# LSTM gate biases as ScalarE operands, one tanh per gate, gate products in two PSUM banks, on a recurrent Trainium2 kernel

## The reference, cut to what matters

```
def _lstm_cell(xt, h, c, wih, whh, b):
    g = xt @ wih + h @ whh + b
    i, f, gg, o = jnp.split(g, 4, axis=1)
    c = sigmoid(f) * c + sigmoid(i) * tanh(gg)
    h = sigmoid(o) * tanh(c)

encoded = tanh(xt @ We + st @ Ue + be)
new_state = tanh(xt @ Wx + st @ Ws + bk)           # eight candidates
mem = concat([encoded, err], mem[:-1])
a = relu(mem.flat @ enc_w1 + enc_b1); agent_in = relu(a @ enc_w2 + enc_b2)
h1, c1 = _lstm_cell(agent_in, h1, c1, ...)         # cell 0 of the kernel
h2, c2 = _lstm_cell(h1, h2, c2, ...)               # cell 1 of the kernel
gate = softmax(h2 @ gate_w + gate_b) * theta + gs * (1 - theta)
st = sum_c gate_c * new_state_c; pred = clamp01(st[-1]); err = pred - yt
```

## Time and profile before

| what | value |
|---|---|
| runs, median (lowest to highest) | 5569.39 us (5567.42 to 5569.56), 3 runs |
| the profiled execution, span of its instructions | 5567.1 us |
| what lies around that span, against the median of the runs | 2.3 us |
| mean granted TensorE clock | 0.998 of full |
| busy: PE, DVE, ACT, POOL | 98%, 84%, 68%, 40% |
| chain that ended last: DVE, PE, ACT, issue | 54%, 19%, 17%, 8% |

### The profile page before, as it was taken

How to read it: one execution, slowest core, us unless ns; L and a number is a source line. 1 busy time by engine, 2 the same in 40 slices (tenths; PEclk the granted TensorE clock), 3 DMA queues, 4 the chain that set the end, 5 groups by cost and what they waited for, 6 DMA issues and landing times.

```text
span 5567.1 us, 187596 instructions
## 1 busy us (share of the span) xinstructions
PE 5448.0 (98%) x67584; PEld 3452.2 (62%) x67584; DVE 4654.7 (84%) x12848; ACT 3792.9 (68%) x9729; POOL 2203.7 (40%) x4101
## 2 busy tenths in 40 slices
PE   8999999999999999999999999999999999999998
PEld 5666666666666666666666666666666666666665
DVE  7888888888888888888888888888888888888887
ACT  5666666666666666666666666666666666666665
POOL 3344444433333344444443333334444444333333
PEclk9999999999999999999999999999999999999999
DMA  2111111111111111111111111111111111111111
GB/s 67 29 31 29 29 31 29 31 28 31 28 31 29 31 29 31 29 29 31 29 31 28 31 28 31 29 31 29 31 29 29 31 28 31 28 31 28 31 29 39
DMA packets 299285, 172.38 MB, mean 31 GB/s; under 512 B 156734, under 2 KB 263882, under 8 KB 298714
## 3 DMA queue, kind: packets, MB, share of 16 engines
q1 hardware_dynamic: 293568, 159.42, 11.0%
q10 hardware_dynamic: 5146, 3.66, 0.2%
HBM read 74.65 MB, written 2.10 MB: 14 GB/s over the span
## 4 chain that ended last, share of the span: by engine, by line
DVE 54%; PE 19%; ACT 17%; issue 8%; DVEq 1%; DMA 0%; ACTq 0%; POOL 0%; POOLq 0%
DVE mixed L802 11%; DVE state L820 11%; PE chain L416 10%; DVE added L719 9%; DVE cell_in L734 8%; PE a_ps L365 5%; ACT cand L553 4%; ACT entry_parts L529 4%; ACT gates L560 2%; ACT entry L516 2%; DVE fresh L784 2%; PE chain L316 2%; DVE total L769 2%; DVE chain L791 2%; DVE recip L774 2%
## 5 line engine op out<-in xcount | busy, mean ns | idle before, releaser
L365 PE MATMUL a_ps<-hist,w_hist 125*64 125x512 f16 x12288 | 1899.7, 383 | 24.1 <-DMA w_hist<-enc_table 24.1
L820 DVE TENSOR_REDUCE state<-mixed 128x64 f32<-128x512 f32 x2048 | 1353.1, 681 | 34.1 <-POOL mixed L916 0.8
L952 POOL COPY preds<-pred_now 128x8 f32 x512 | 101.0, 197 | 3064.1 <-DVE pred_now L828 3064.1
L916 POOL TENSOR_TENSOR mixed<-cand,gate 128x512 f32<-128x512 f32 x1024 | 1283.9, 1275 | 48.6 <-POOL gate L904 12.5
L416 PE MATMUL chain<-cell_in,cell_w 128*64 128x128 f32 x16384 | 1121.4, 278 | 70.9 <-DVE cell_in L734 18.1
L416 PEld LDWEIGHTS chain<-cell_in,cell_w 128*64 128x64 f32 x16384 | 889.2, 136 | 384.8 <-DVE cell_in L734 313.5
L553 ACT ACTIVATE cand<-cand_ps 128x512 f32<-128x512 f32 x2048 | 1101.6, 592 | 1.6 <-PE cand_ps L346 1.2
L560 ACT ACTIVATE gates<-chain 128x384 f32<-128x384 f32 x1024 | 502.0, 490 | 840.2 <-PE chain L416 840.2
L365 PEld LDWEIGHTS a_ps<-hist,w_hist 125*64 125x64 f16 x12288 | 693.0, 109 | 524.2 <-issue 141.3
L719 DVE SCALAR_TENSOR_TENSOR added<-gates 128x256 f32<-128x256 f32 x1024 | 638.5, 624 | 172.6 <-ACT gates L560 172.6
L734 DVE SCALAR_TENSOR_TENSOR cell_in<-gates,tanh_c 64x128 f32<-64x128 f32 x2048 | 581.7, 284 | 206.2 <-ACT tanh_c L570 192.5
(11 more groups left out here) (76 smaller groups left out, 6541.2 us busy)
## 6 DMA issues: line engine op xcount, KB each, us to landing
x_sb<-in_x_l SPq DMA_DIRECT2D x260, 256.0 KB, 2.7
hist<-entry_parts SPq DMA_DIRECT2D x2048, 25.0 KB
w_hist<-enc_table SPq DMA_DIRECT2D x258, 128.0 KB, 2.4
y_rows<-in_y_l SPq DMA_DIRECT2D x260, 8.0 KB
ys<-in_y ACTq DMA_DIRECT2D x1, 2048.0 KB, 16.7
preds_out<-preds SPq DMA_DIRECT2D x1, 2048.0 KB, 7.5
cand<-in_encoder ACTq DMA_DIRECT2D x1, 640.0 KB, 3.8
cell_w<-in_cell ACTq DMA_DIRECT2D x2, 256.0 KB, 4.6
```

The lines of the kernel that those rows point to most:

```text
L365: nc.tensor.matmul(a_ps[g][ENC * half:ENC * half + ENC, :], w_hist[0:HROWS, w_slot(u), kk, wp, :], hist[0:HROWS, xp, k, at:at + 512], star ...
L820: V.tensor_reduce(state[:, g, hf, 2 * pair:2 * pair + 2, :], mixed[:, pair, hf, :, :, :], AX, ALU.add)\
L916: G.tensor_tensor(mixed[:, 0, :, q, :, :], cand[:, g, 0, :, q, :, :], over_s, ALU.mult)\
```

## The change

Biases. The bias matmuls of the cells (`bias_of_cell`) go, with `indicator`, `cell_bias` in fp16, its staging and its low part. The biases are eight columns of `columns` instead, given to ACT's tanh as its `bias` operand, one for each cell and gate.

Gates. `cell_tanhs` was one instruction; it is three of 128 columns now (input, forget, new), each with a bias column, and `cell_tanh_out` is a fourth. Input and forget products are written into columns 0 to 255 of `chain`, new and output products into columns 0 to 255 of `a_ps`. PE writes input and forget first and raises `q_cps_if`, then new and output and raises `q_cps_go`. In cell 0 the input and forget tanhs are written back in place, in PSUM, and DVE's `cell_terms` reads them there; in cell 1 they go to `gates[1]` in SBUF as before.

Hidden state. The two copies of `next_hidden` on ACT become one on POOL, 128 by 256, after its two mixes. `agent_input` on ACT and on DVE waits for it (`q_hnext`) in place of PE's `cell_gates`.

PE's `logit_bias` goes ahead of `history_waits` and `history(new, 0, 0, 1)`, since `a_ps` must be read before that writes it. Setup loses one DMA on ACT's queue for the staged biases, one for the indicator and one on SP's, and three small DVE operations; it gains two.

```diff
+OUT_GATE, IN_GATE, FORGET_GATE, NEW_GATE = range(4)
+IN_CHAIN, IN_A = (IN_GATE, FORGET_GATE), (NEW_GATE, OUT_GATE)
...
+        cell_bias = [[columns[:, 6 + 4 * c + r:7 + 4 * c + r] for r in range(4)] for c in range(2)]
...
-            def bias_of_cell(item, c):
...
-                for rows in CELL0_OUT:
-                    nc.tensor.matmul(chain[g][rows, :], cell_bias[:, c, rows], indicator[:, :],
-                                     start=True, stop=False, skip_group_check=True)
+            def gate_at(g, r):
+
+                bank, place = (chain[g], IN_CHAIN.index(r)) if r in IN_CHAIN else (a_ps[g], IN_A.index(r))
+                return bank[:, P * place:P * place + P]
 
             def cell_gates(item, c):
                 g, n, u = item
                 if c == 0:
                     pe.wait_ge(q_in, n)
                     pe.wait_ge(q_in_high, n)
-                    pe.wait_ge(q_hnext, n)
                 else:
                     pe.wait_ge(q_h[0], n)
-                for r in range(4):
+                for r in IN_CHAIN + IN_A:
                     for hf in range(HF):
                         rows = (CELL0_OUT, CELL1_OUT)[c][hf]
-                        last = nc.tensor.matmul(chain[g][rows, P * r:P * r + P], cell_w[c][:, hf, r, :],
-                                                cell_in[c][:, g, hf, :], start=False, stop=True,
+                        last = nc.tensor.matmul(gate_at(g, r)[rows, :], cell_w[c][:, hf, r, :],
+                                                cell_in[c][:, g, hf, :], start=True, stop=True,
                                                 skip_group_check=True)
-                last.then_inc(q_cps[c], 1)
+                    if r == IN_CHAIN[-1]:
+                        last.then_inc(q_cps_if[c], 1)
+                    if r == IN_A[-1]:
+                        last.then_inc(q_cps_go[c], 1)
...
                     encoded_s(cur)
+                if old:
+                    logit_bias(old)
                 if new:
                     history_waits(new, extra)
                     history(new, 0, 0, 1)
                 if cur:
                     history(cur, 3, 1, 2)
-                if old:
-                    logit_bias(old)
...
                     encoder1_now(cur)
-                    bias_of_cell(cur, 0)
...
-                    bias_of_cell(cur, 1)
                     cell_gates(cur, 1)
...
             def agent_input(item, hf):
                 g, n, u = item
                 rows = AGENT_ROWS[hf]
+                act.wait_ge(q_hnext, n)
                 act.wait_ge(q_inps, n)
...
             def cell_tanhs(item, c):
                 g, n, u = item
-                act.wait_ge(q_cps[c], n)
-                nc.scalar.activation(gates[c][:, g, 1:4, :].rearrange("p r b -> p (r b)"), chain[g][:, P:4 * P],
-                                     ACT.Tanh).then_inc(q_gates[c], 1)
+
+                act.wait_ge(q_cps_if[c], n)
+                for place, r in enumerate(IN_CHAIN):
+                    at = chain[g][:, P * place:P * place + P]
+                    nc.scalar.activation(at if c == 0 else gates[c][:, g, r, :], at, ACT.Tanh,
+                                         bias=cell_bias[c][r][:, 0:1])
+                act.wait_ge(q_cps_go[c], n)
+                at = P * IN_A.index(NEW_GATE)
+                nc.scalar.activation(gates[c][:, g, NEW_GATE, :], a_ps[g][:, at:at + P], ACT.Tanh,
+                                     bias=cell_bias[c][NEW_GATE][:, 0:1]).then_inc(q_gates[c], 1)
 
             def cell_tanh_out(item, c):
                 g, n, u = item
-                nc.scalar.activation(gates[c][:, g, 0, :], chain[g][:, 0:P], ACT.Tanh).then_inc(q_out_gate[c], 1)
+                at = P * IN_A.index(OUT_GATE)
+                nc.scalar.activation(gates[c][:, g, OUT_GATE, :], a_ps[g][:, at:at + P], ACT.Tanh,
+                                     bias=cell_bias[c][OUT_GATE][:, 0:1]).then_inc(q_out_gate[c], 1)
...
-            def next_hidden(item, hf):
-                g, n, u = item
-                rows = CELL0_OUT[hf]
-                if hf == 0:
-                    act.wait_ge(q_h[0], n)
-                last = nc.scalar.activation(cell_in[0][rows, g, hf, :], cell_in[1][rows, g, hf, :], ACT.Copy)
-                if hf == HF - 1:
-                    last.then_inc(q_hnext, 1)
...
                 if new:
                     encoder1(new)
-                if cur:
-                    next_hidden(cur, 0)
-                if new:
                     agent_input(new, 0)
                     cell_tanhs(new, 0)
-                if cur:
-                    next_hidden(cur, 1)
-                if new:
                     cell_tanh_out(new, 0)
...
             def cell_terms(item, c):
                 g, n, u = item
                 dve.wait_ge(q_gates[c], n)
-                V.scalar_tensor_tensor(added[c][:, g, :, :], gates[c][:, g, 1:3, :], 1.0,
-                                       gates[c][:, g, 3:5, :], ALU.add, ALU.mult).then_inc(q_added[c], 1)
+                if c == 0:
+                    shares = chain[g][:, 0:2 * P].rearrange("p (r b) -> p r b", b=P)
+                else:
+                    shares = gates[c][:, g, 1:3, :]
+                V.scalar_tensor_tensor(added[c][:, g, :, :], shares, 1.0, gates[c][:, g, 3:5, :],
+                                       ALU.add, ALU.mult)\
+                    .then_inc(q_added[c], 1)
...
             def agent_input(item, hf):
                 g, n, u = item
                 rows = AGENT_ROWS[hf]
+                dve.wait_ge(q_hnext, n)
                 dve.wait_ge(q_inps, n)
...
+            def next_hidden(item):
+
+                g, n, u = item
+                pool.wait_ge(s_ready, 1)
+                pool.wait_ge(q_h[1], n)
+                G.tensor_copy(cell_in[0][:, g, :, :], cell_in[1][:, g, :, :]).then_inc(q_hnext, 1)
+
...
                     mix_quarter(old, 1)
                     mix_quarter(old, 0)
+                    next_hidden(old)
                     keep_prediction(old, extra)
```

More of the change, by code:

```diff
@@ L38, with recurrent_kernel @@
 FIRST_HALF = (0, 0)
+OUT_GATE, IN_GATE, FORGET_GATE, NEW_GATE = range(4)
+IN_CHAIN, IN_A = (IN_GATE, FORGET_GATE), (NEW_GATE, OUT_GATE)
 PIECES = ((0, 0), (1, 0), (0, 1))
 assert 1 + LOOPS * PER_TILE == STEPS and HT * PER_TILE == MEM
-def recurrent_kernel(nc, x_l, y_l, y, error0, gate0, w, ident_c, columns_c, ind_c, out):
+def recurrent_kernel(nc, x_l, y_l, y, error0, gate0, w, ident_c, columns_c, out):
     ctx = ExitStack()
@@ L56, in recurrent_kernel @@
         ident = sb("ident", [P, P])
-        columns = sb("columns", [P, 6])
+        columns = sb("columns", [P, 6 + 2 * 4])
         set_scale = [columns[:, c:c + 1] for c in range(2)]
         err_rows, be_col, enc1_bias, enc2_bias = (columns[:, c:c + 1] for c in range(2, 6))
-        indicator = sb("indicator", [P, 512], FP16)
+        cell_bias = [[columns[:, 6 + 4 * c + r:7 + 4 * c + r] for r in range(4)] for c in range(2)]
         ones16 = sb("ones16", [P, P], FP16)
@@ L73, in recurrent_kernel @@
         gate_w = sb("gate_w", [P, HF, Q * C])
-        bias_stage = sb("bias_stage", [4, 2, P])
-        bias_low = sb("bias_low", [4, 2, P], FP16)
-        cell_bias = sb("cell_bias", [P, 2, P], FP16)
         gate_bias_stage = sb("gate_bias_stage", [1, TILES * C])
@@ L140, in recurrent_kernel @@
         q_mul = [sem(f"q_mul{pair}") for pair in range(2)]
-        q_cps, q_gates, q_added, q_cell, q_tanhc, q_h = (
+        q_cps_if, q_cps_go, q_gates, q_added, q_cell, q_tanhc, q_h = (
             [sem(f"q_{n}{c}") for c in range(2)]
-            for n in ("cps", "gates", "added", "cell", "tanhc", "h"))
+            for n in ("cps_if", "cps_go", "gates", "added", "cell", "tanhc", "h"))
         (q_hnext, q_logps, q_peak, q_logit, q_exp, q_total, q_recip, q_share, q_fresh, q_gate,
@@ L216, in _ @@
             sp.wait_ge(s_parts, 1)
-            sp.dma_start(cell_bias[4:8, :, :], bias_low[0:4, :, :]).then_inc(s_fix, 16)
             sp.dma_start(gate_bias[1:2, :], gate_bias_low[0:1, :]).then_inc(s_fix, 16)
@@ L285, in _ @@
             pe.wait_ge(s_ready, 1)
-            pe.wait_ge(s_fix, 16 * 3)
+            pe.wait_ge(s_fix, 16 * 2)
             def state_transpose(item, hf):
@@ L494, in _ @@
             act.dma_start(enc1_stage, w["encoder"]).then_inc(s_table, 16)
-            act.dma_start(bias_stage[:, :, :].rearrange("r n b -> r (n b)"), w["biases"]).then_inc(s_biases, 16)
             act.dma_start(gate_bias_stage[:, :], w["gate_b"]).then_inc(s_biases, 16)
@@ L501, in _ @@
             load(gate_w[:, :, :].rearrange("p h c -> p (h c)"), w["gate_w"])
-            load(indicator[:, :], ind_c)
             load(gate[:, :, :, :], gate0.rearrange("(g j p) c -> p g j c", g=GROUPS, p=P))
@@ L627, in _ @@
             V.memset(ones16[:, :], 1.0)
-            V.memset(cell_bias[:, :, :], 0.0)
             V.memset(gate_bias[:, :], 0.0)
@@ L640, in _ @@
             dve.wait_ge(s_prep, 1)
```

(17 more changed lines are left out.)

7 lines of the change are left out of this document (removed).

## The result

The changed kernel takes 5519.19 us (median of 4 runs, 5518.67 to 5521.54) against 5568.98 us before: ratio 0.9912, 95% interval 0.9900 to 0.9925, some 50 us faster. The forecast was 5515 us, in a range of 5490 to 5545.

What follows compares the result with a forecast made beforehand. The loop through DVE (route D) bounds the kernel; after the change ACT's path does. 512 x 0.08 = 41, turns 12 and setup 1 take 54 from 5567: 5513 profiled, 5515 us as median, range 5490 to 5545.

Steps and rivals of the forecast that it cites:

- The stall of L719: DVE's L719 in cell 0 waits for POOL's mixes; reading PSUM makes it 0.42 instead of 0.78 us.
- route D: Path through DVE and h of cell 0 between agent_inputs; no slack before, h 0.35 us earlier after the change.
- R1: Rival, slower: ACT's biased tanhs don't overlap, step 0.385 us; about 5700 us, chance 0.16.
- R2: Rival, faster: ACT's bias fetch hides wholly under the preceding tanh, step 0.18 us; about 5430 us, chance 0.08.
- R3: Rival, slower: POOL's long copy takes the port ahead of cell 0's L725; about 5615 us, chance 0.08.
- Wrong if: Signs against: L725 of cell 0 well over 0.29, steps 0.38, DVE's wait not growing, PE late though h is there.
- DVE's wait for cell 1's gates: Expected sign on DVE: this wait grows from 0.33 to about 0.6 us.
- part 4: Copy of h moves from ACT to POOL, assumed 0.43 us long; new q_hnext waits stop nobody; worth 0.
- both routes: Paths between agent_inputs through DVE (route D) and through ACT's candidates (0.38 us slack), said to be one from cell 1's tanh.
- route E: Not in the prediction; named in follow-ups: from cell 0's h through PE's gates, transposes and encoding, then ACT's encoded, to encoder1_now.
- Turns: Two long beats in each of 51 turns; the second loses 0.23 us, the first stays: 12 us gained.
- the setup: Setup ahead of the beats: fewer small operations, none over 1 us, worth 1 us.

Runs made afterwards that it cites:

- e1: Changed kernel with cell 0's input and forget tanhs written to SBUF again and read there by DVE: 5601.78 us.
- e12: e1 with POOL's copy of h also held back until h of the next beat's cell 0: 5564.61 us.
- e3: Kernel before the change, without the two cells' bias matmuls (their biases not added): 5563.93 us, ratio 0.9996.
- e7: Kernel before the change, with one extra 128-column ACT tanh a beat just before cell 1's tanh: 5572.86 us, ratio 1.0008.
- e9: Changed kernel with the same extra ACT tanh in the same place as e7: 5619.42 us.
- e4: Changed kernel without the bias operands on the gate tanhs of both cells (biases not added): 5482.67 us.
- e8: e4 with POOL's copy of h also held back until h of the next beat's cell 0: 5399.60 us.
- e5: Changed kernel with only POOL's copy of h held back until h of the next beat's cell 0: 5519.74 us.
- e14: Changed kernel, copy left on POOL, waits for q_hnext moved one instruction earlier on ACT and DVE, third wait added on PE's gates: 5496.95 us.
- e13: Changed kernel with the two copies of h back on ACT and the waits for q_hnext back on PE: 5464.46 us, ratio 0.9808.

## Why the prediction was right, and where its terms were off

**Right in kind.** The forecast was 3.7 us below the measured median. The stall of L719 was POOL's (e1, e12); the PSUM operand removes it (0.425 in all 512 beats); the removed matmuls alone are worth nothing (e3); the gain stops at ACT, whose three biased tanhs use up 0.38 us of slack (e7, e9), and doesn't reach the 0.35 of route D. That shortening ACT's tanhs shortens the beat (e4, e8) says the same from the other side. ACT's wait ahead of cell 1's tanhs went to zero as said. R1 (no overlap) fell with steps of 0.25 us; R2 fell too, since they aren't 0.18; R3's mechanism is real at 0.41 us and was covered (e5). So one of the signs that I had put under "Wrong if" did come, cell_value of cell 0 well over 0.29, without its price; as a sign it was too strict, since it looks at a length and not at what waits for it. Another sign fell short: DVE's wait for cell 1's gates grew from 0.33 to 0.41, not to 0.6, as h of cell 0 gained 0.15 and not 0.35.

**The sum, term by term.** Predicted: 0.08 a beat. An ordinary beat went from 10.724 to 10.663 us on average, 0.06. Cut at the same events, the two kinds of ordinary beat side by side (medians over all beats of a kind):

| stretch (us) | before | after | forecast |
|---|---|---|---|
| agent_input starts to candidates start on ACT | 3.55, 3.55 | 3.60, 3.60 | no change |
| to cell 1's new value | 2.47, 2.45 | 2.35, 2.35 | 0.08 less |
| to the end of `errors` | 2.20, 2.27 | 2.20, 2.27 | no change |
| to encoder1 | 1.26, 1.19 | 1.19, 1.19 | no change |
| to agent_input starts | 1.25, 1.25 | 1.29, 1.29 | no change |

The second row is the forecast's own, 0.12 instead of 0.08: the step was 0.25 and not 0.265, and the first tanh started 0.13 ahead of the candidates' end and not 0.10. The first and the last are the step that failed, in part 4 ("the two new waits for `q_hnext` stop nobody"): they stop nobody, but their form costs 0.06 and 0.04 us a beat. The fourth row is a gain that I hadn't counted, 0.08 in every other beat, and it comes from another hole in the prediction: it says that from cell 1's tanh onward both routes are one. They aren't. In those beats PE's `encoder1_now` waited for `encoded`, at the end of route E, which ended within 0.01 of `errors`; now it ends 0.09 ahead. So 0.12 + 0.04 - 0.10 = 0.06, 31 us over 512 beats, where 41 were forecast.

**Turns.** Forecast 12 us, with one long beat of 0.24 left. The excess per turn fell from 0.47 us to 0.15, 16 us. Together that is the 47 us by which the span shrank, where 54 were forecast; for the 1 us that the prediction gave to the setup nothing is left.

**Smaller misses.** h of cell 0 came at 3.90, not 3.69: L704 started at 1.92 instead of 1.84, since cell 0's new value was ready late, at 1.89 rather than 1.7, and L711 lost 0.13 to the copy. Both lay in the slack behind h, so the time didn't show them, but the slack was narrower than I had it: about 0.07 us a beat until route E takes over (e4), not the 0.27 that lie between my 0.35 and 0.08. R1's price has a slip: by its own numbers new ends 6.02 - 5.72 = 0.30 late, not 0.28, which is 154 us and not 143; its verdict is the same.

**Luck.** The mechanism was right, but the time came nearer than its terms: the handovers cost some 50 us that the forecast put at nothing, and the larger gain in its own row, the gain in route E and the one in the turns gave back most of it.

## What to carry to other kernels

Where routes through the engines are close, undoing the part that shows in the trace says little by itself: the same hold on the copy was worth 0 and 83 us, depending on the other route; pair each edit with a test that adds a known instruction to the route thought critical. Give a VectorE instruction that runs beside GpSimd at most one SBUF operand, and put GpSimd's other work where VectorE doesn't take two. Look for the second way behind a value, too: an engine that goes through its list in order passes a delay on to whatever stands next in it. At a handover on the critical route look at which of several waits ends last: with the long-done wait of `agent_input` on an earlier instruction, and a third one behind PE's two, both gaps closed (e14).

## What the runs showed of the hardware that I hadn't expected

- At a handover with several waits the gap depends on which of them ends last. With a long-done wait ahead of the real one `agent_input` started 0.127 us after encoder2's end on ACT and 0.141 on DVE, with the real one alone (e13, e14) 0.067 and 0.069. PE's gates of cell 0 started 0.139 after `agent_input` with two waits, 0.083 and 0.080 with a third, long-done one behind them. PE's `encoder1_now` has two waits in every kernel, `errors` and then `encoded`: it started 0.077 after the end when `errors` ended last (changed kernel) and 0.144 when `encoded` did (e4). All of these fit one reading, that it is slow where the wait that ends last is also the last of several in the program. No run changed only the order of two waits, so that stays a reading.
- Of the biased tanhs of 128 columns of cell 0, written back in place to PSUM, the first two took 342 and 333 ns; the same two written to SBUF (e1) took 367 and 359. In cell 1, to SBUF, they took 382 to 399. The two in-place ones overlap by 0.07 (step 0.27), but the third, to SBUF, didn't overlap the second (2513.50, two of them 0.60, the next from 2514.11); with all three to SBUF the step there was 0.25 (e1), as between the three of cell 1.
- At POOL's port a copy of POOL's that was next in its queue went ahead of a VectorE instruction that came just after it, and VectorE's length then grew from 0.29 to between 0.43 and 0.51: it ended 0.14 after the copy did (2515.40 against 2515.26; the same in e4 and e14).
